# A graph block on one core: the feed-forward weights are turned by the DMA that reads them back from DRAM instead of on TensorE

## The reference, cut to what matters

```python
def lpbq_dequant(w):                      # BLOCK = 32, W_BITS = 4
    O, I = w.shape
    wb = w.reshape(O, I // BLOCK, BLOCK)
    s = max(max(abs(wb), axis=-1) / 7, 1e-12)
    return (clip(round(wb / s), -8, 7) * s).reshape(O, I)

xn = layernorm(x)
x = x + gnn(xn, src, dst) + mix(xn)
xf = act_qdq(layernorm(x))                # 16-bit codes, one scale per tensor
up = act_qdq(xf @ lpbq_dequant(w_up).T)   # w_up, w_gate: (384, 1024)
gate = act_qdq(xf @ lpbq_dequant(w_gate).T)
gate = act_qdq(gate * fixed_qdq_u16(sigmoid(gate)))
out = x + act_qdq(gate * up) @ lpbq_dequant(w_down).T   # w_down: (1024, 384)
```

## Time and profile before

| | us |
|---|---|
| median of 3 executions | 1229.46 |
| lowest, highest | 1228.35, 1230.82 |
| the profiled execution | 1228.89 |
| its span, first to last instruction | 1226.8 |

### The profile page before, as it was taken

How to read it: one execution, slowest core, us unless ns; L and a number is a source line. 1 busy time by engine, 2 the same in 40 slices (tenths; PEclk the granted TensorE clock), 3 DMA queues, 4 the chain that set the end, 5 groups by cost and what they waited for, 6 DMA issues and landing times.

```text
span 1226.8 us, 15391 instructions
## 1 busy us (share of the span) xinstructions
PE 1158.0 (94%) x6376; PEld 626.4 (51%) x6376; DVE 688.6 (56%) x1234; ACT 354.9 (29%) x441; POOL 386.2 (31%) x226
## 2 busy tenths in 40 slices
PE   3898899999999999999999999999999999969958
PEld 2554455555555554444444555444444445559823
DVE  6769669656274583249225345656664355672663
ACT  5533343333423323322411111312110012253430
POOL 2167566768677674678100000000000000000000
PEclk7998999999999999999999999999999999989979
DMA  9843653342432438632620225213220030000014
GB/s 263 312 120 54 173 156 72 56 108 20 91 68 42 108 71 253 181 79 97 255 93 1 72 104 178 86 35 137 69 103 18 36 153 1 1 1 2 1 33 134
DMA packets 138574, 117.62 MB, mean 96 GB/s; under 512 B 74796, under 2 KB 113964, under 8 KB 137480
## 3 DMA queue, kind: packets, MB, share of 16 engines
q1 hardware_dynamic: 69192, 103.44, 25.6%
q0 software_dynamic: 69024, 13.07, 8.2%
q10 hardware_dynamic: 288, 0.13, 0.0%
HBM read 94.85 MB, written 21.41 MB: 95 GB/s over the span
## 4 chain that ended last, share of the span: by engine, by line
PE 87%; DVE 7%; issue 3%; ACT 2%; DMA 1%; POOL 0%; SPq 0%; POOLq 0%; ACTq 0%; DVEq 0%
PE ps L1030 33%; PE ps L949 27%; PE ps L1092 7%; PE ps L1064 7%; PE ps L1117 6%; PE ps L1137 3%; DVE key_b L1219 2%; DMA raw<-in_L_gnn_W_self_dram 1%; PE ps L936 1%; DVE whl L1201 1%; PE ps L1009 1%; PE ps L1080 1%; PE ps L913 0%; PE ps L957 0%; DVE xnT L1207 0%
## 5 line engine op out<-in xcount | busy, mean ns | idle before, releaser
L582 POOL DMA_INDIRECT at_scratch<-copies,cell x160 | 338.0, 2113 | 174.8 <-DMA at_scratch<-copies,cell 104.5
L949 PE MATMUL ps<-xnT,whl 128*128 128x512 f16 (+1 forms) x2160 | 385.9, 342 | 5.0 <-DVE T L1299 5.0
L949 PEld LDWEIGHTS ps<-xnT,whl 128*128 128x128 f16 x2160 | 211.8, 99 | 176.9 <-issue 9.8
L1030 PE MATMUL ps<-hb,hT 128*128 128x512 f16 x960 | 209.1, 379 | 1.3 <-DVE hT L1488 1.3
L1030 PEld LDWEIGHTS ps<-hb,hT 128*128 128x128 f16 x960 | 93.6, 98 | 112.3 <-DVE hT L1488 1.8
L1030 PE MATMUL ps<-hb,VT 128*128 128x512 f16 x480 | 103.9, 379 | 1.5 <-ACT S_b L724 1.5
L563 POOL PARTITION_ALL_REDUCE ag_fw<-am_fw x9 | 3.2, 356 | 323.2 <-DVE am_fw L1356 323.2
L1030 PE MATMUL ps<-hb,xnT 128*128 128x512 f16 x480 | 104.2, 379 | 0.0
L1092 PE MATMUL ps<-P,AT 125*128 125x512 f16 x400 | 87.8, 379 | 0.0
L1064 PE MATMUL ps<-AT,P 125*128 125x512 f16 (+1 forms) x480 | 84.7, 339 | 0.0
L1030 PEld LDWEIGHTS ps<-hb,VT 128*128 128x128 f16 x480 | 46.9, 98 | 58.0 <-ACT S_b L724 1.9
(11 more groups left out here) (223 smaller groups left out, 1188.3 us busy)
## 6 DMA issues: line engine op xcount, KB each, us to landing
raw<-in_L_gnn_W_neigh_dram SPq DMA_DIRECT2D x32, 512.0 KB
raw<-in_L_gnn_W_self_dram SPq DMA_DIRECT2D x24, 512.0 KB
key_b<-key_scratch SPq DMA_DIRECT2D x8, 1250.0 KB, 11.7
raw<-in_L_mix_Wo_dram SPq DMA_DIRECT2D x16, 512.0 KB
parts<-at_scratch POOLq DMA_DIRECT2D x20, 312.5 KB, 4.5
at_scratch<-zeros POOLq DMA_DIRECT2D x6, 1020.0 KB, 17.9
x_all<-in_x_dram SPq DMA_DIRECT2D x9, 512.0 KB
x_acc<-in_x_dram SPq DMA_DIRECT2D x9, 512.0 KB
```

The source lines that it names most:

```text
L582: pool.indirect_dma_start(out=at_scr[c % 2][:, :], out_offset=bass.IndirectOffsetOnAxis(ap=cell[:, c:c + 1], axis=0), in_=copies[:, c:c + ...
L949: mm = pe.matmul(acc_of(c)[:, a:b], whl[:, i, wp, k, :], xnT[:, k, ap, a:b], start=(k == 0 and wp == 0 and ap == 0), stop=(k == KC - 1 and ...
L1030: mm = pe.matmul(half_bank(i), stationary[:, k, ap, t * TP:t * TP + P], hb[:, n % 2, k, wp, :], start=(k == 0 and wp == 0 and ap == 0), st ...
```

## The change

TensorE's transposes, VectorE's copy and `wst` go. SP stores `fw16` as it is, once its low part is written, and the loads back become transposing DMAs: the stored row p of chunk j, seen as 16 blocks of 128, is written so that block b's element n lies on partition n, block b, place p. ScalarE, which overwrites `fw16` for chunk j, waits for the stores of all chunks before it. `ident16` and its two GpSimd instructions go too.

```diff
             for n in (4, 5, 6, 7):                         # SP
                     if j is not None:
-                        sp.wait_ge(fwt_free, j + 1)
-                        sp.dma_start(w_scr[j], wst[:, :, :].rearrange("p s d -> p (s d)")).then_inc(wst_out, 16)
+                        worked(sp, at["ffn", j])
+                        sp.dma_start(w_scr[j], fw16[:, :, :, :].rearrange("p s k n -> p (s k n)")).then_inc(wst_out, 16)
             sp.wait_ge(wst_out, 16 * NF)
             sp.wait_ge(mm_done, 80)
             for j in (3, 6, 4, 7, 5, 8, 0, 1, 2):
                 to = w_last[:, :, :] if j == NF - 1 else w8[:, j, :, :]
-                sp.dma_start(to.rearrange("p s d -> p (s d)"), w_scr[j]).then_inc(w9_in[j], 16)
+                sp.dma_start_transpose(to.rearrange("p s (k n) -> p (s k) n", n=P), w_scr[j]).then_inc(w9_in[j], 16)
...
-            steps(pool.memset(ident16[:, :], 0.0))
-            pool.affine_select(out=ident16[:, :], in_=ident16[:, :], compare_op=ALU.not_equal, fill=1.0,
-                               base=0, pattern=[[-1, P]], channel_multiplier=1)
...
                 if j > 0:                                  # ScalarE, ffn_hi(j)
-                    act.wait_ge(fwt_done, j)
+                    act.wait_ge(wst_out, 16 * j)
...
-            def turn_ffn(j):
-                r = at["ffn", j]
-                worked(pe, r)
-                if j == 0:
-                    pe.wait_ge(so_ok, WS1 + 1)
-                else:
-                    pe.wait_ge(fwt_free, j)
-                for part in range(2):
-                    for k in range(KC):
-                        o = 6 * 1024 + part * D + k * P
-                        mm = pe.transpose(ps16[:, o:o + P], fw16[:, part, k, :], ident16[:, :])
-                mm.then_inc(fwt_done, 1)
...
-                    if i in turn_at:                       # half_product
-                        turn_ffn(turn_at[i])
...
                 if t == 0:                                 # turn_x2
-                    pe.wait_ge(fwt_free, NF)
+                    pe.wait_ge(so_ok, WS1 + 1)
...
-            def ffn_turned(j):
-                dve.wait_ge(fwt_done, j + 1)
-                if j > 0:
-                    dve.wait_ge(wst_out, 16 * j)
-                dve.tensor_copy(wst[:, :, :].rearrange("p s d -> p (s d)"),
-                                ps16[:, 6 * 1024:8 * 1024]).then_inc(fwt_free, 1)
```

More of the change, by code:

```diff
@@ L143, in build @@
         fw16 = sb("fw16", [P, 2, KC, P], F16, RG)
-        wst = sb("wst", [P, 2, D], F16, RG + 4096)
         b1_b = sb("b1_b", [P, D], F32, RG)
@@ L168, in build @@
         const = Area(RZ, 229312)
-        ident16 = const("ident16", [P, P], F16)
         ident32 = const("ident32", [P, P], F32)
@@ L267, in build @@
         b1_ok, m1_ok, gelu_ok = sem("b1_ok"), sem("m1_ok"), sem("gelu_ok")
-        fw_max, fw_all, fw_s, fw_hi, fwt_done, fwt_free = (
-            sem(n) for n in ("fw_max", "fw_all", "fw_s", "fw_hi", "fwt_done", "fwt_free"))
+        fw_max, fw_all, fw_s, fw_hi = (sem(n) for n in ("fw_max", "fw_all", "fw_s", "fw_hi"))
         ag1_done, ag1_half, ag1_free = sem("ag1_done"), sem("ag1_half"), sem("ag1_free")
@@ L1415, in _ @@
                         job(("half", WO_, 1, j))
-            def turned(i):
-                if i - 1 in turn_at:
-                    ffn_turned(turn_at[i - 1])
             def behind_tile(i):
@@ L1518, in _ @@
                     weight_scale(W_SUMS[i - 1])
-                turned(i)
                 behind_tile(i)
```

## The result

| | before | changed |
|---|---|---|
| median, us | 1229.36 (4 executions) | 1219.78 (4 executions) |
| lowest, highest | 1228.35, 1230.82 | 1219.65, 1220.10 |
| the profiled execution, its span | 1228.89, 1226.8 | 1219.83, 1218.0 |

The ratio is 0.9924, with a 95% interval of 0.9911 to 0.9936. That is 9.6 us less where 8.6 were forecast.

The account below looks back on a forecast made before the run. TensorE alone was taken to bound the stretch from 770.17 to 980.24 us. Profiled 1228.89 - 8.04 - 0.57 + 0 = 1220.28; from the median 1229.46 - 8.61 = 1220.85, say 1220.8, range 1218.8 to 1223.2.

Parts of the forecast that it names:

- The turns: Nine groups of 16 transposes on TensorE, 770.17 to 980.24 us: all on the path, removing them gives -8.04 us.
- The copies: VectorE's nine copies of 1.214 us, 10.9 us in all: VectorE waits for TensorE there, so worth 0.
- The start: Two GpSimd instructions for `ident16` go, so `once` is selected earlier: -0.57 us, bounds -0.6 and +0.4.
- The loads back: Nine transposing loads, each taking t, from 980.3 us: t between 1.44 and 9.3 us, all in time, cost 0.
- Rival A: Gate group 0 waits for serial transposing loads, costing from 18.1 us a chunk; 1394 us at 41.6 a chunk; chance 0.05.
- Rival B: Transposing loads delay instruction fetches on the DMA engines: up to 28 us in the second aggregation, 1248 us; chance 0.04.
- Rivals C and D: C: something else holds tile stream's pace, 1228.9, chance 0.04; D: slow transposing loads hidden in part, 1221 to 1229, chance 0.02.
- The new wait on the stores: ScalarE's `ffn_hi(j)` waits for earlier stores; tightest at `ffn_hi(3)` with 5 to 6 us left: cost 0, upper bound 1.

## Why the prediction was right, point by point

- **The turns, -8.04.** Right to the hundredth: 210.07 became 202.03, and putting the turns back gave 210.07 again. The difference of the starts in the chain, not the 219 ns of a transpose in its row, was the price to use.
- **The copies, 0.** Right for the span, and shown alone: 10.9 us of copies cost nothing there. The sum took the 2.09 us outside the span as fixed; with the copies gone they are 1.83 (last section).
- **The start, -0.57.** This step failed. The mechanism on GpSimd is there (the select of `once` came first, the signal earlier), but the step from there to 131 us took a chain from one execution for a fixed sum. The chain passes a DMA and TensorE's clock steps, and for unchanged code the products end anywhere within 3.3 us. The bounds of -0.6 and +0.4 were therefore bounds of the edit and no bounds of what a profile shows. L1071 starts at 972.54, 7.70 us before the old 980.24, and not 8.6. The medians moved by 9.58 us where 8.61 were forecast; the profiled executions by 9.06, of which 8.80 lie in the span. Beside the 8.04 these are the other rows of the table above: 0.41 less at the start, 0.75 more up to tile 40, then 0.69 and 0.42 less in the gate, up and down stages. With the +0.01 they add up to -0.76, near the forecast -0.57, and that is luck. Eleven other profiles show the first 288 products at 52.29 to 53.69 us (52.14 before, 52.89 changed), and eleven show the first gate group's 72 matmuls, with no edit there, at 9.17 to 10.62 us (9.91 before, 9.21 changed). So both differences are no larger than those between runs of like code. About 0.3 of the medians' 9.58 lies outside the span. Which part of the rest is chance can't be told from four executions.
- **The loads back, t between 1.44 and 9.3.** Right: 2.55 us a chunk. The picture of 2048 packets of 256 bytes fits, with 32 more, but the packet was mis-sized: 21 ns and not 72.6, which was a mean over packets of 1.5 KB. The time to landing was forecast at 10 to 84 us and is 4.4 to 6.3: the forecast had all nine issued at once, but SP takes some 2.4 us to issue each, nearly the 2.55 us of a chunk. One margin was miscounted: up's chunks are needed 145 us after the first issue (1125.26 - 980.3), not 150, which changes nothing here. The Trainium skill's page "DMA: Bandwidth & Descriptors", section "Latency and other measured facts", gives 261 GB/s where the middle dimension is not contiguous, which the prediction used without that condition, and about 350 to 400 where it is; here 524288 bytes in 2.55 us are 206 GB/s, below both. The Trainium skill's 1309 ns for one block ("VectorE: DVE Perf Modes", section "The three transpose paths") is no price for a block in such a load: here 16 blocks take 2.55 us in a stream, 0.16 us each, and 4.8 us from issue to landing when a load is awaited. No run turned one block alone. Nor does a row show the same table's 390 ns on TensorE: it is 219 ns from issue to end and 56 ns from one to the next.
- **Rival A, the load back as the wait.** Place, price and point of decision held when it was forced: 108 us to the third gate chunk, and 23.4 us of wait with the sixth chunk issued 126.8 us after the first. Its formula was too strict by one pace: the sixth chunk is in time if five paces and one landing fit, not six, as the run with four more loads showed. It also left out the 1.7 us that the clock adds behind the pause.
- **Rival B, the instruction fetch.** In the changed kernel one fetch falls into the stream of the nine loads (between 980 and 990 us), and TensorE has no gap there. With four more loads behind each, nine fetches fall into 188 us at a DMA share of 0.61, and the second aggregation has no gap either. Fetches in a long stream at 0.98 were not tried.
- **Rivals C and D.** Both are out: TensorE's stretch is shorter by all of the 8.04 us, and 2.55 us a chunk is far under 18.1.
- **The new wait on the stores, cost 0.** Right, with more room than given. The tightest case was computed with the loads where they stood before; but without the wait for the copy, SP issues them earlier as well, and store 2 went out at 831.22 us and not after 837.9, with `ffn_hi(3)` at 847.11. It landed 6.9 us later, at 838.1 (4.3 us was the longest that the prediction counted with), so the slack was 9.0 us, not 5 to 6.

The sum was off by little, since its wrong terms, the start and the fixed 2.09 us outside the span, are small: what decided was the 8.04 us.

## What to carry to other kernels

Where one engine has the chain without a gap, price an operation there by the difference of the starts around it, and take work off that engine even if another path, such as a transposing DMA, takes more time for the same job: it needs to be in time, not fast. Work out how late it may be from the first use of each piece and the order of the queue, and add what the lower clock behind a pause costs. A term under a microsecond read from one profile's chain through DMAs and clock steps is no term until the same code has been seen twice.

## What the runs showed of the hardware that was not expected

**A second chain lies just under the first.** The changed kernel, run again, had an execution of 1224.29 us and a span of 1222.5. Tiles 41 to 79 took 202.03 us as always, but began at 773.23: the stretch from `S_b` to there took 311.41 us, where the first profile has 307.03. Its chain of waits, read back from there, leaves TensorE at 573.70 for VectorE, and goes back to GpSimd's scatter of the count matrix:

```profile
550.01 3.73 DMA at_scratch<-copies,cell
...
554.96 3.71 DMA parts<-at_scratch
...
571.25 2.41 DVE hb L1322
...
573.70 49.66 PE ps L1011 x222
```

The last of 160 scatters was issued at 550.0 us; in the other profiles that is 534.0 to 546.9, and TensorE waits for nothing there. VectorE then waited 10.85 us for the first part of the matrix, and the addition behind it took 10.18 us where the next one of the same shape took 0.80. The timeline of VectorE, and one row of GpSimd's:

```profile
558.69 10.18 DVE L1215 TENSOR_TENSOR AT<-parts 128x1250 f16<-128x1250 f16 x1 [10.85 <-DMA parts<-at_scratch]
...
574.82 0.80 DVE L1215 TENSOR_TENSOR AT<-parts 128x1250 f16<-128x1250 f16 x1
```

```profile
556.62 11.58 POOL L603 TENSOR_TENSOR x_acc<-x_acc,b_b 125x1024 f32<-125x1024 f32 x5
```

The long addition is not special to this execution. In twelve of the fourteen profiles it takes 8.67 to 10.52 us, and in each of them it begins during GpSimd's run of five additions and ends 0.67 to 0.69 us after it (here 568.87 against 568.20). In the other two (the turns back, two more loads) it begins over 2 us after a run of GpSimd's has ended, and takes 0.80 us. So it goes with GpSimd's work; no run was made to show why. GpSimd starts those five behind the scatter, and this time all of it came late enough to reach TensorE, which lost 2.64 us to the wait; from 573 to 580 us its granted clock was 0.76, and 311.41 - 307.03 - 2.64 leaves 1.74 us for that. It is a possible source of the single executions of up to 1228.22 us, but only this one was profiled.

**About 0.3 us outside the span.** Between the span and the whole execution lie 2.09 us in the kernel before and 1.83 in the changed one. The other executions settle where it comes from. Beside the experiments the kernel before has 2.08 to 2.20 us there in all 37 executions, and with the copies back it is 2.10 to 2.18 in all four. In every other version it is 1.76 to 1.88, the ten executions with the turns back among them (1.78 to 1.85). So the 0.3 us goes with the nine copies on VectorE and their waits, and not with the turns, the stores or the identity. It is part of the gain, and too small for the medians to show. Why instructions that cost nothing inside the span lengthen the time outside it stays open.
